# Feed-forward with FP4 codes: four codes transposed as one 32-bit word, scales turned on VectorE and spread by DMA, rows normalised on ScalarE

## What is computed

```python
def fp4_quant_dequant(x):                     # blocks of 16 along the last dimension
    xb = x.reshape(shape[:-1] + (shape[-1] // BLOCK, BLOCK))
    scale = jnp.maximum(jnp.max(jnp.abs(xb), axis=-1, keepdims=True) / 6.0, 1e-12)
    xn = xb / scale
    q = _GRID[jnp.searchsorted(_MID, jnp.abs(xn))] * jnp.sign(xn) * scale   # grid 0 .. 6
    return q.reshape(shape)
def fp4_linear(x, w):
    return jnp.einsum('bsk,nk->bsn', fp4_quant_dequant(x), fp4_quant_dequant(w))
x = x + attention(layernorm(x))
y = layernorm(x)
h = jax.nn.silu(fp4_linear(y, w_gate)) * fp4_linear(y, w_up)          # 1408 hidden features
x = x + fp4_linear(h, w_down)
```

## Time and profile before

| | us |
|---|---|
| median of 3 runs | 3051.26 (3050.97 to 3052.3) |
| time of the profiled execution | 3052.97 |
| its span, first to last instruction | 3051.2 |
| TensorE / VectorE busy | 2989.1 (98%) / 2622.9 (86%) |
| ScalarE / GpSimd busy | 1350.4 (44%) / 755.0 (25%) |

### The profile page before, as it was taken

One profiled execution on the slowest core, in us unless ns is written; L12 is line 12 of the kernel. 1 busy time (PEld: TensorE's weight loads), 2 busy tenths in 40 slices (PEclk: granted clock), 3 DMA queues, 4 the chain that ended last, 5 costly groups with the idle time before them and its releaser, 6 DMA issues.

```text
span 3051.2 us, 65181 instructions
## 1 busy us (share of the span) xinstructions
PE 2989.1 (98%) x23204; PEld 2208.6 (72%) x23204; DVE 2622.9 (86%) x4209; ACT 1350.4 (44%) x2010; POOL 755.0 (25%) x680
## 2 busy tenths in 40 slices
PE   7999899999999999889999999999999999999999
PEld 6787644444444444478888888888888888888887
DVE  7999788889889888888888888888888888888886
ACT  5666577877777787532222222222222222222221
POOL 3444200000000000023333333333333333333332
PEclk9999899999999999999999999999999999999999
DMA  7889856655655665521111111111111111101110
GB/s 244 283 289 300 275 123 143 149 133 137 154 133 138 149 137 137 151 84 32 38 42 42 42 35 35 42 41 42 42 33 36 42 42 41 42 30 40 42 35 15
DMA packets 247628, 304.20 MB, mean 100 GB/s; under 512 B 21968, under 2 KB 154960, under 8 KB 247504
## 3 DMA queue, kind: packets, MB, share of 16 engines
q1 hardware_dynamic: 247504, 302.88, 35.8%
HBM read 190.35 MB, written 112.46 MB: 99 GB/s over the span
## 4 chain that ended last, share of the span: by engine, by line
PE 56%; DVE 1%; ACT 0%; DMA 0%; issue 0%; POOL 0%; SPq 0%; DVEq 0%
PE p_ring L1845 20%; PE p_ring L1873 16%; PE ps_od L1845 11%; PE ps_od L1825 5%; PE p_ring L1863 3%; PE p_ring L1853 1%; DVE sb_wg_lo L1751 0%; PE ps_od L1873 0%; PE p_ring L1825 0%; PE p_ring L1888 0%; DVE sb_fp_tmp L102 0%; DVE sb_wd_lo L1751 0%; DMA dn<-sb_fp_tmp 0%; DVE sb_h_amax L88 0%; DVE sb_stage L1722 0%
## 5 line engine op out<-in xcount | busy, mean ns | idle before, releaser
L1040 ACT ACTIVATE sb_probs<-scores 128x1024 f32<-128x1024 f32 (+3 forms) x512 | 405.8, 840 | 113.7 <-PE scores L1246 107.3
L788 POOL TENSOR_TENSOR sb_at_in<-sb_at_in,sb_inv_in 128x512 f32<-128x512 f32 x64 | 89.0, 1390 | 1069.0 <-DMA sb_inv_in<-dinv 1068.3
L1845 PE MATMUL p_ring<-sb_wg_hi,sb_xq_hi 128*128 128x512 f32 (+1 forms) x1024 | 295.2, 369 | 0.3 <-DVE sb_wd_lo L1751 0.3
L1548 POOL TENSOR_TENSOR sb_stage<-sb_stage,sb_h_inv 128x512 f32<-128x512 f32 (+1 forms) x192 | 210.8, 1098 | 339.2 <-DVE sb_h_inv L94 339.2
L1845 PE MATMUL p_ring<-sb_wg_lo,sb_xq_hi 128*128 128x512 f32 (+1 forms) x1024 | 290.5, 365 | 0.0
L1845 PE MATMUL p_ring<-sb_wg_hi,sb_xq_lo 128*128 128x512 f32 (+1 forms) x1024 | 289.9, 364 | 0.0
L1873 PE MATMUL p_ring<-sb_wd_hi,sb_ht_hi 128*128 128x512 f32 x693 | 275.9, 398 | 0.0
L1246 PEld LDWEIGHTS scores<-sb_q_hi,sb_k_hi 32*128 32x128 f32 x1536 | 73.7, 182 | 278.3 <-ACT sb_probs L1040 154.6
L1873 PE MATMUL p_ring<-sb_wd_hi,sb_ht_lo 128*128 128x512 f32 x693 | 270.2, 390 | 0.0
L1873 PE MATMUL p_ring<-sb_wd_lo,sb_ht_hi 128*128 128x512 f32 x693 | 269.8, 389 | 0.0
L1554 POOL TENSOR_TENSOR sb_stage<-sb_stage,sb_h_scale 128x512 f32<-128x512 f32 (+1 forms) x192 | 190.0, 989 | 267.4 <-DVE sb_stage L104 267.4
(11 more groups left out here) (203 smaller groups left out, 7172.3 us busy)
## 6 DMA issues: line engine op xcount, KB each, us to landing
kq<-sb_kq_out SPq DMA_DIRECT2D x32, 1024.0 KB, 7.2
sb_kq_raw<-kq SPq DMA_DIRECT2D x64, 512.0 KB, 6.8
sb_xin<-in_L_attn_x_dram SPq DMA_DIRECT2D x32, 512.0 KB, 6.9
v<-sb_v_out SPq DMA_DIRECT2D x64, 256.0 KB, 6.5
rq<-sb_r_out SPq DMA_DIRECT2D x64, 256.0 KB, 4.4
sb_qr<-rq SPq DMA_DIRECT2D x32, 512.0 KB
sb_kr_hi<-kr SPq DMA_DIRECT2D x32, 512.0 KB
sb_kr_lo<-kr SPq DMA_DIRECT2D x32, 512.0 KB
```

The source lines that it names most:

```text
L1040: act.activation(probs(k)[:, 2 * pair:2 * pair + 2, off:BANK], scores[(2 * k + pair) % RING2][:, :, off:BANK], ACT.Exp, scale=SCALE).then_ ...
L1548: pool.tensor_tensor(x, x, spread(h_inv[:, a // QB:b // QB], (b - a) // QB), ALU.mult).then_inc(h_y, 1)
L1845: i = pe.matmul(ps[:, m, 0:b0 - a0], xt[a][:, c, :], wg[b][:, m, c, a0:b0], start=(c == 0 and a == b == 0), stop=(c == DC - 1 and a == 1))
```

## The change

A quantised value is a small whole number of half scales, from -12 to 12. The changed kernel doesn't transpose values but these numbers. The rounding now works with half scales times 2^23 (`fp4_half_scales`), ScalarE turns its result into one byte, number + 64 (`code_x`, `code_hidden`), and four bytes that lie beside each other are one 32-bit word. TensorE transposes the words: one block for x, three for h (two in `HT0`, one in `HT1`). The features are therefore spread over the words as 4a + c, and the weight blocks are turned with the same stride. VectorE reads the bytes from PSUM, takes 64 off and multiplies by the scales in one instruction (`decode`). For this the scales must lie across the rows: VectorE transposes them in blocks of 32x32, SyncE stores them to memory (16 KB each) and loads them back, each row to four partitions (or 16 for the last slice). The rounded part is then copied from SBUF by ScalarE, and the rest taken from SBUF by VectorE. The products with the scales on VectorE and GpSimd (`hidden_q`) fall away. ScalarE normalises the rows (`normalise`), for which GpSimd computes -mean times rstd (`shift`). x is loaded straight into `x1` instead of `x_in`. GpSimd's `divide` stands behind `hidden_y(0)`, and the rest of the attention at the end.

```diff
+def fp4_half_scales(dve, x, amax, scale, inv, sem, base):
...
+    dve.tensor_scalar(scale, amax, SIXTH / 2, MIN_SCALE / 2, ALU.mult, ALU.max).then_inc(sem, 1)
...
+    dve.tensor_scalar(inv, inv, TIES / CODE_STEP, None, ALU.mult).then_inc(sem, 1)
...
+    def load_x(self, sp, b, j):
...
+        sp.dma_start(self.x1[:, j % 4, :], self.x_v[b, j]).then_inc(self.x_loaded[i], 16)
...
             sp.wait_ge(ps_free, number(0, -1, "WO") + RING3 + 1)
             sp.wait_ge(last_stored, 32)
             ahead.load_chunk(sp, 2 * B - 1)
+            ahead.load_x(sp, 0, 1)
             ahead.load_tile(sp, 0, 2)
             sp.wait_ge(ahead.at_divided, 2)
             ahead.load_inverse(sp, 0, 2)
 
             def body(b, j):
                 q, r = b * HALF + j // UNROLL3, j % UNROLL3
+                if exists(q, r + 2):
+                    sp.wait_ge(stored[(r + 2) % 4], count(q, (r + 2) // 4 * 4, 4, 16))
+                    ahead.load_x(sp, b, j + 2)
...
-                if exists(q, r - 1):
-                    store(b, j - 1)
+                if exists(q, r + 1):
+                    store_x_scale(q, r + 1)
+                    spread_x_scale(q, r + 1)
+                for s in range(2):
+                    spread_h_scale(q, r, s)
                 if exists(q, r + 3):
                     sp.wait_ge(ahead.at_divided, count(q, r, 1, 3))
                     ahead.load_inverse(sp, b, j + 3)
+                spread_h_scale(q, r, 2)
+                if exists(q, r - 1):
+                    store(b, j - 1)
...
+                pool.wait_ge(ln_steps, count(q, r, 3, 2))
+                pool.tensor_tensor(negmean[:], moments[:, 0:1], minus[:], ALU.mult).then_inc(s_rstd, 1)
                 pool.wait_ge(ln_steps, count(q, r, 3, 3))
                 pool.tensor_tensor(rstd[:], vareps[:], mhalf[:], ALU.pow).then_inc(s_rstd, 1)
+                own(pool, s_rstd, count(q, r, 3, 3))
+                pool.tensor_tensor(shift[:], negmean[:], rstd[:], ALU.mult).then_inc(s_rstd, 1)
...
-            def hidden_q(q, r, s):
...
-                pool.tensor_tensor(x, x, spread(h_scale[:, a // QB:b // QB], (b - a) // QB), ALU.mult).then_inc(h_q, 1)
...
             def body(q, r):
                 if exists(q, r + 1):
                     inverse_deviation(q, r + 1)
+                hidden_y(q, r, 0)
                 if exists(q, r + 2):
                     divide(q, r + 2)
-                hidden_y(q, r, 0)
...
+                hidden_y(q, r, 1)
+                hidden_y(q, r, 2)
                 if exists(q, r + 2):
                     rest_of_attention(q, r + 2)
-                hidden_y(q, r, 1)
-                hidden_q(q, r, 0)
-                hidden_y(q, r, 2)
-                hidden_q(q, r, 1)
-                hidden_q(q, r, 2)
...
+                act.wait_ge(s_rstd, count(q, r, 3, 4))
+                act.activation(xq[:], x1[:, r % 4, :], ACT.Identity, bias=shift[:], scale=rstd[:]).then_inc(x_normed, 1)
...
+            def code_x(q, r):
+                act.wait_ge(x_chain, count(q, r, X_STEPS, X_STEPS))
+                act.activation(x_codes[:].bitcast(U8), xq[:], ACT.Identity, bias=code_zero[:],
+                               scale=CODE_STEP).then_inc(x_coded, 1)
...
+            def code_hidden(q, r, s):
...
+                act.activation(out, codes, ACT.Identity, bias=code_zero[:], scale=CODE_STEP).then_inc(h_coded, 1)
...
             def round_x(q, r, it):
-                act.wait_ge(ps_ready, number(*it, "XT") + 1)
-                act.copy(xt_hi[:], ring[where(*it, "XT")][:, 0, :].rearrange("p (c q) -> p c q", c=DC)).then_inc(x_hi, 1)
+                act.wait_ge(ps_free, number(*it, "XT") + RING3 + 1)
+                act.copy(xt_hi[:], x_values).then_inc(x_hi, 1)
...
             def body(q, r):
                 first = flags(q, r)[0]
+                following = exists(q, r + 1)
+                if following:
+                    normalise(q, r + 1)
                 if exists(q, r - 1):
                     round_hidden(q, r, 0)
                 if first:
                     for n in range(GATE_JOBS, 25):
                         round_job(n)
-                if exists(q, r + 1):
+                if following:
...
+                magic_h(q, r, 0)
+                if following and not first:
+                    code_x(q, r + 1)
                 silu_of(q, r, 1)
-                magic_h(q, r, 0)
+                code_hidden(q, r, 0)
...
                     round_x(q, r + 1, (q, r))
                 magic_h(q, r, 2)
+                code_hidden(q, r, 1)
...
+                code_hidden(q, r, 2)
...
-                dve.wait_ge(stored[r % 4], count(q, r // 4 * 4, 4, 16))
-                dve.wait_ge(in_loaded[r % 2], count(q, r // 2 * 2, 16, 32))
+                dve.wait_ge(ahead.x_loaded[r % 2], count(q, r // 2 * 2, 8, 16))
...
-                dve.wait_ge(s_rstd, count(q, r, 1, 2))
-                dve.tensor_scalar(xq[:], x1[:, r % 4, :], moments[:, 0:1], rstd[:], ALU.subtract,
-                                  ALU.mult).then_inc(x_chain, 1)
-                own(dve, x_chain, n + 1)
-                fp4_scales(dve, xq[:], x_amax[:], x_scale[:], x_inv[:], x_chain, n + 1)
-                own(dve, x_chain, n + 1 + SCALES_STEPS)
+                dve.wait_ge(x_normed, count(q, r, 1, 1))
+                fp4_half_scales(dve, xq[:], amax[:], x_scale[:], x_inv[:], x_chain, n)
+                own(dve, x_chain, n + SCALES_STEPS)
+                dve.transpose(x_turned[:], x_scale[:]).then_inc(x_turned_done, 1)
                 x = blocks_of(xq[:])
                 dve.tensor_tensor(x, x, spread(x_inv[:], D // QB), ALU.mult).then_inc(x_chain, 1)
...
                 dve.wait_ge(x_magic, count(q, r, 1, 1))
-                fp4_round(dve, xq[:], x_big[:], tmp[:], x_chain, n)
-                own(dve, x_chain, n + ROUND_STEPS)
-                x = blocks_of(xq[:])
-                dve.tensor_tensor(x, x, spread(x_scale[:], D // QB), ALU.mult).then_inc(x_chain, 1)
-            def rest_of_x(q, r, it):
-                dve.wait_ge(x_hi, count(q, r, 1, 1))
-                dve.tensor_tensor(xt_lo[:], ring[where(*it, "XT")][:, 0, :].rearrange("p (c q) -> p c q", c=DC),
-                                  xt_hi[:].bitcast(F32), ALU.subtract).then_inc(ps_free, 1)
+                fp4_round(dve, xq[:], x_big[:], xq[:], x_chain, n)
...
+            def decode(out, words, scales):
+                return dve.scalar_tensor_tensor(out=out, in0=bytes_of(words)[:, 0:out.shape[1]],
+                                                scalar=CODE_ZERO, in1=scales, op0=ALU.subtract, op1=ALU.mult)
...
+            def decode_x(q, r, it):
...
-                dve.tensor_tensor(h[:, a:b], ps[:, 1, 0:b - a], silu[:, h_slot(r, s), 0:b - a],
-                                  ALU.mult).then_inc(ps_free, 1)
+                dve.tensor_tensor(h[:, a:b], ps[:, 1, 0:b - a], h[:, a:b], ALU.mult).then_inc(ps_free, 1)
...
+                dve.transpose(h_turned[:, s], h_scale[:, s * P // CODES:(s + 1) * P // CODES]).then_inc(h_turned_done, 1)
...
+            def decode_hidden(q, r, j):
+                dve.wait_ge(h_spread_loaded[j], count(q, r - 1, (32, 48)[j], (32, 48)[j]))
+                ps = read_out(q, r, f"HT{j}")
+                if j == 0:
+                    for s in range(2):
+                        i = decode(h_values[:, CODES * s:CODES * s + CODES], ps[:, 0, s * P:s * P + P],
+                                   shared(h_spread[s]))
+                else:
+                    i = decode(rest_q, ps[:, 0, 0:P], h_spread[2])
+                i.then_inc(ps_free, 1)
+            def rest_of_x(q, r):
+                dve.wait_ge(x_hi, count(q, r, 1, 1))
+                dve.tensor_tensor(xt_lo[:], x_values, xt_hi[:].bitcast(F32), ALU.subtract).then_inc(x_rest, 1)
             def rest_of_hidden(q, r, j):
 
                 a, b = HT_CHUNKS[j]
-                dve.wait_ge(ht_rounded, count(q, r - 1, 2, j + 1))
-                src = ring[where(q, r, f"HT{j}")][:].rearrange("p s (c q) -> p (s c) q", q=P)
-                dve.tensor_tensor(ht_lo[:, a:b], src[:, 0:b - a], ht_hi[:, a:b].bitcast(F32),
-                                  ALU.subtract).then_inc(ps_free, 1)
+                dve.wait_ge(ht_rounded, count(q, r, 2, j + 1))
+                dve.tensor_tensor(ht_lo[:, a:b], values(j), ht_hi[:, a:b].bitcast(F32), ALU.subtract).then_inc(ht_rest, 1)
...
             def body(q, r):
                 following = exists(q, r + 1)
@@ -1769,32 +1927,38 @@
                 if following:
                     residual(q, r + 1, (q, r))
                 if exists(q, r - 1):
-                    rest_of_hidden(q, r, 0)
+                    decode_hidden(q, r, 0)
                 if first:
                     for n in range(GATE_JOBS, 24):
                         rest_of_job(n)
                 if following:
                     x_to_y(q, r + 1)
+                if exists(q, r - 1):
+                    rest_of_hidden(q, r - 1, 0)
```

(25 more changed lines are left out.)

183 lines of the change are left out of this document (139 added, 44 removed).

## The result

The changed kernel takes 3032.54 us (median of 4, 3031.18 to 3034.2) against 3051.11 before: a ratio of 0.9938 with a 95% interval of 0.9924 to 0.9953. It is 0.6% faster, where 1.6% was forecast. The profiled execution has a span of 3030.2 us, 21.0 less than before.

A forecast was written before the change was run, and what follows sets the result against it. TensorE was taken to bound the feed-forward at 27.02 us a tile. A beat of 26.07 gives -59 us, start +9, end +2, preparation -1: from 3052.97 to 3005, 3003 us for the median; range 2984 to 3048.

The forecast's parts named there:

- TensorE spared: Feed-forward tile on TensorE: eleven fewer transposes at 0.092 us each save 1.01 us, giving a tile of 26.0 us.
- VectorE's additions and removals: VectorE's tile: -1.30 us for normalisation and scale product, +2.27 for four decodes, +0.5 for four scale transposes.
- rival B: VectorE becomes the bound through slow byte decodes or turned scales: beat 26.3 to 26.9, 3014 to 3045 us; chance 0.24.
- The stalls by GpSimd: VectorE instructions held up beside GpSimd's: 3.1 us a tile before, 2.7 after, so -0.4.
- The loop: Loop through TensorE and VectorE: 10.3 us for down and output projection plus 15.5 for VectorE's part, so 25.9 a tile.
- forecast A: The study's own forecast: beat of 25.95 to 26.2 us, 2992 to 3014 us in all; chance 0.52.
- The signs: What would show it: TensorE busy over 99%, VectorE over 93%, ScalarE wait before L1839; TensorE gaps over 20 us refute.
- Scales by DMA at no cost: Scales stored and spread back in about 6 us, wanted 10 us later; cost nothing if both steps stay under 5 us.
- rival C: Scales come late by DMA, decode_hidden and TensorE wait: beat 27.1 at 5 us a step, 31 at 6; chance 0.11.
- Start +9: Start of the stage: x of tile 1 loads behind the job loads, delaying residual, normalise and TensorE; +9 us.
- The preparation: In the preparation VectorE no longer waits for the last store: -1 us.
- End +2: End of the stage: the last tile's path gets decodes and a second copy, less the 3.6 us of before: +2 us.

The follow-up runs named there:

- e8: Changed kernel with a 128x1 constant allocated behind the transposed hidden values and GpSimd's divide ahead of the product of slice 0: 2992.7 us.
- e4: Changed kernel with GpSimd's divide ahead of the product of slice 0 again, as in the kernel before: 3005.6 us.
- e1: Changed kernel with one 128x1 constant allocated behind the transposed hidden values instead of ahead of them: 3020.7 us.
- e2: Kernel before with an unused 128x1 tensor ahead of the transposed hidden values, which start 32 bytes further on: 3068.2 us.
- f1: e8 with an unused 128x1 tensor ahead of the down projection's weights, so both its operands start 32 bytes further: 3010.1 us.
- f3: e8 with an unused 128x32 tensor behind the down projection's weights, so transposed x and hidden values start 128 bytes further: 3017.7 us.
- e7: e4 with the transpose of the words of x done four times instead of once, the three more unread: 3023.6 us.
- e9: Changed kernel with the normalisation on VectorE again, as in the kernel before, in place of ScalarE's: 3029.9 us.

## Why the prediction missed, step by step

- **TensorE spared, 1.01 us a tile: low; it is 1.19.** With nothing else in the way (e8) the beat is 27.02 - 25.83 = 1.19 less. The price of 0.092 was a mean over 15 transposes, but the ones that stay cost less than those that went: from start to start XT fell from 0.35 to 0.03 (e4), HT0 from 0.79 to 0.14, HT1 from 0.24 to 0.03, 0.11 for each of the eleven. That "TensorE's tile would be 26.0" and e4 has 26.03 is luck: 0.18 more spared and 0.2 more for the slower down projection cancel.
- **VectorE's additions and removals: right.** A decode takes 0.69 us and 0.60 to the next start, a turned scale 0.20 and 0.13, the values taken. VectorE waits 31.1 / 59 = 0.53 us a tile for the output projection, so its own tile is 26.48 - 0.53 = 25.95, where 26.0 was forecast. So it isn't the bound by itself: 3032.5 us lies in the range of rival B, but B's reason, slow decodes or slow turned scales, didn't occur.
- **The stalls by GpSimd: right in size.** L118 and L120 of x lose 0.5 + 1.0 us, as laid out, and VectorE's part of the loop, 15.65 us, was added up at 15.5; its terms aren't listed, but stalls of 1.5 can hardly have been left out of it. What the prediction didn't ask is which stall costs time. That of x lies in the loop: taking the divide out of it gave 0.46 us a tile (e4). That of `round_hidden(1)` beside the rest of the attention (1.67 us at 2006.28) lies behind it, and VectorE still waits for the output projection afterwards.
- **The loop, 25.9 us: the step that failed.** It is 26.48. 0.21 is the down projection and the output projection, 10.54 against 10.33 us, which I took over unchanged; their instructions are the same, but the addresses aren't (e1, e2, f1 to f3). Some 0.18 are the handovers, 0.25 us against some 0.07, and 0.15 is VectorE's part. "Three bounds lie within 0.1, so small delays will show" was right, but then 0.07 above the highest of them was far too little, and the range of forecast A was too narrow: 0.42 us a tile on 61 tiles are 26 of the 29.5 us missed.
- **The signs.** TensorE was busy in 99.4% of the stretch, as forecast, and its gaps sum to 9.8 us, under the 20 that were to say that the forecast is wrong. Both signs read the modelled ends, which hide most of the wait; from start to start it is 0.4 us a tile. VectorE was busy in 91.8%, not in over 93%. The wait for ScalarE stands before L106 and not before L1839.
- **Scales by DMA at no cost: right.** 4.6 us for both steps, rival C had no part. The stores with rows of 128 bytes, of which the Trainium skill (DMA: Bandwidth & Descriptors, "Specifications") speaks, land within 2.5 us (1990.84 to 1993.31, issue included), where 0.4 + 1.6 was reckoned with: they aren't doubled.
- **Start +9: right for its reason, +11.05 measured;** the rest of the attention on GpSimd is the part not seen. The preparation gave 2.35 where 1 was forecast, but that isn't shown: in the runs that keep the changed preparation the projection of tile 1 starts between 1298.10 (e7) and 1301.24 us (f3), and in e2, which has the old one, at 1299.41.
- **End +2: +3.4.** The path to the last down projection is as forecast: from the last tile's first transposes to it 6.17 us instead of 3.96, 2.2 more, with a wait of 5.68 us instead of 2.18. From there to the end it is 12.78 us instead of 11.04, since the granted clock after the wait is 0.50 (1.2 GHz) where it was 1.00: the first seven steps take 3.12 us, where seven at 0.2333 take 1.63. The clock's drop after a wait was booked at the start of the stage and forgotten here. It isn't the change's alone: e2, the kernel before but for addresses, waits 2.33 us at this place and has the same 0.50 and 3.12 us behind it. The first of these matmuls in the kernel before and in the changed one, and the stretch table of the seven steps of the latter:

```profile
3040.14 0.47 PE L1873 MATMUL ps_od<-sb_wd_hi,sb_ht_hi 128*128 128x512 f32 x1 [2.18 <-DVE sb_ht_lo L1740]
```

```profile
3017.43 0.77 PE L2034 MATMUL ps_od<-sb_wd_hi,sb_ht_hi 128*128 128x512 f32 x1 [5.68 <-DVE sb_ht_lo L1898]
```

```profile
3017.43:3020.55 3.12, 3.12 (x7) 2.45 (x8) 0.00 (x0) 0.00 (x0) 0.00 (x0) 0.50 0.02 5
```

## What to carry to other kernels

When a change takes the bound off one engine, add up the loops through two engines with every handover, and weigh each stall by whether it lies in the loop; then put work that is free to move (here GpSimd's divide) beside an instruction that it doesn't slow, or beside a wait. Before a saving of 1% is believed, look whether the instructions that stayed still have their old step: a constant of four bytes a partition cost 12 us here (e1). Measure an engine's idle time from start to start where its ends are modelled. A work unit moved to another engine is worth only what its wait leaves over (e9).

## What the runs showed of the hardware

In these kernels a matmul of the down projection (128x512) steps at 0.2275 us when the start addresses of its moving and stationary operands in SBUF lie a multiple of 512 bytes apart, and at about 0.2333 us at distances of 32, 96 or 128 more. Gate and up lose about 0.1 us on the 24 matmuls of a slice at 32, 64 and 128 more. The place itself isn't what counts: 32 bytes off for both is fast (f1), a multiple of 128 for both at another distance is slow (f3). The Trainium skill (SBUF — State Buffer, "A bandwidth-pool intuition that's wrong") gives weight loads an independent read port beside that of the moving operand; from that one wouldn't expect a step that depends on the distance between the two, and the runs show one. Whether the ports have a part in it is not shown.
